# Last FFN: VectorE adds the right tap through PSUM, ScalarE rounds in two activations

## The chip, the core and the metric

The kernel runs on one NeuronCore of a Trainium2 chip. TensorE (PE in the profile) multiplies matrices and writes into PSUM, VectorE (DVE) and GpSimd (POOL) do elementwise work and reductions, ScalarE (ACT) evaluates activations, SyncE (SP) issues most of the DMAs. GpSimd cannot reach PSUM. Every engine runs its own instructions in order, and the engines hold each other back only by semaphores. The metric is the device time of one execution in microseconds, median of several runs.

## The reference, cut to what matters

The kernel computes one decoder layer on x of 4 x 1024 x 512 (4096 tokens): x = x + attention(norm(x)), x = x + cross block(norm(x), ctx), x = x + ffn(norm(x)). The change lies in the last of the three:

```python
def _L0_ffn_ref(x, w1, conv_w, conv_b, w2):      # w1 2048x512, w2 512x2048
    def act_quant(x):
        scale = 127.0 / jnp.clip(jnp.max(jnp.abs(x), axis=-1, keepdims=True), 1e-05)
        return jnp.clip(jnp.round(x * scale), -128, 127) / scale
    ...
    h = bit_linear(x, w1)                        # both operands quantised, then x @ w1.T
    h = depthwise_conv1d(h.transpose(0, 2, 1), conv_w, conv_b)   # 3 taps along the tokens
    h = h.transpose(0, 2, 1)
    h = jax.nn.silu(h)
    return bit_linear(h, w2)
```

Each token's scale needs the largest |h| over all 2048 hidden columns before h can be rounded and multiplied by w2.

## The kernel before, in words

The program is a chain of stages. The last, `quantised_ffn`, finds the rounded x, both rounded weights and their units ready in DRAM. It works on half a sequence at a time: 8 units of 512 tokens, each with 16 blocks of 128 hidden columns, so 128 blocks of 128 partitions (hidden columns) x 512 tokens. A block i passes these steps:

- PE `block_product` (L2411): four matmuls of 512 columns into `acc`, two PSUM banks in turn.
- DVE `dequantise` (L2534): `acc` times the tokens' units gives `y`, two buffers.
- ACT `set_edge` (L2488): one column of `y`; ACT `centre` (L2495): middle tap plus bias, into PSUM; ACT `right_tap` (L2499).
- DVE `add_left` (L2543): left tap plus `centre` gives `conv`; POOL `add_right` (L2375): plus `right_tap`.
- ACT `silu` (L2479): `conv` gives `h`, kept for two whole units.
- PE `turn` (L2420): four transposes of `h` into `turned`, one PSUM bank with no second buffer; DVE `find_max` (L2551): the largest of each token in the block.
- After a unit's 16 blocks DVE `scales` (six small instructions up to `diag`, L2557 to L2568), PE `spread_scale` (L2428) and an ACT copy (L2513) make `scale_row`.
- POOL `scale_block` (L2381): `h` times `scale_row`; DVE `round_block` (L2576): adds and takes away 1.5 x 2^23, written as bf16 into `hqT`; PE `w2_product` (L2438); DVE `finish` (L2584) once in four blocks.
- Every second unit PE has 128 one-column products for the next sequence's edges (L2402).

All engines are written by the same loop over slots s. In slot s each engine handles block s - lag of each of its steps, with the lags in a few constants, and the order inside a slot is the order of the calls. In slot s PE runs `block_product(s)`, a `w2_product`, and `turn(s - TURN_AT)`; DVE runs `find_max(s - MAX_AT)`, `dequantise(s)`, `add_left(s - 1)`, `round_block`. Buffers tie the blocks: `turn(i)` waits for `maxed` of block i - 1, since `turned` has one buffer:

```python
pe.wait_ge(silu_done, i + 1)
past(pe, maxed, i)
```

and `dequantise(i)` waits for `h_ready` of block i. PE reaches `block_product(s + 1)` only when it is through with `turn(s - TURN_AT)`.

Of the kernel before, what the change touches and what calls it, by code (L numbers as in the profile page):

```python
# [27 lines left out]
ALU = mybir.AluOpType  # L28
# [3 lines left out]
P = 128  # L32
# [2203 lines left out]
def quantised_ffn(nc, ident, w1T_parts, conv_w, conv_b, w2T_parts, w_mean, x2_rows, xq_parts, x_units, out_rows):  # L2236
# [9 lines left out]
    SILU_AT, TURN_AT, MAX_AT = 3, 4, 5  # L2246
    SPREAD_AT, SCALE_AT, ROUND_AT = HB + 5, HB + 6, HB + 7
# [3 lines left out]
    with ExitStack() as ctx:  # L2251
# [13 lines left out]
        right_tap = sb("right_tap", [P, 2, HALF])  # L2265
# [23 lines left out]
        centre_ready, right_ready = sem("centre_ready"), sem("right_ready")  # L2289
# [4 lines left out]
        h_scaled_ready, hq_ready = sem("h_scaled_ready"), sem("hq_ready")  # L2294
        out_ready, out_done = sem("out_ready"), sem("out_done")
# [26 lines left out]
        with nc.Block() as block:  # L2322
# [37 lines left out]
            def _(pool):  # L2360
# [3 lines left out]
                pool.memset(ones[:, :], 1.0).then_inc(const_step, 1)  # L2364
                for s in range(2):
                    pool.memset(y[:, 0, s, 0:1], 0.0).then_inc(const_step, 1)
                    pool.memset(y[:, 1, s, HALF + 1:], 0.0).then_inc(const_step, 1)
                pool.wait_ge(small_loaded, 32)
                pool.wait_ge(const_step, 5)
                pool.sem_inc(const_step, 1)  # L2370

                def add_right(i):
                    pool.wait_ge(right_ready, i + 1)
                    pool.wait_ge(left_added, i + 1)
                    pool.tensor_tensor(conv[:, i % CR], conv[:, i % CR], right_tap[:, i % 2], ALU.add).then_inc(right_added, 1)  # L2375

                def scale_block(i):
                    u, f = divmod(i, HB)
                    pool.wait_ge(scale_row_ready, u + 1)
                    past(pool, hq_ready, i - 1)  # L2380
                    pool.tensor_tensor(h_scaled[:, i % 2], h[:, u % 2, f], scale_row[:, u % 2], ALU.mult).then_inc(h_scaled_ready, 1)  # L2381

                for s in range(END):
# [3 lines left out]
                    i = block_at(s, 1)  # L2387
                    if i is not None:
                        add_right(i)

            @block.tensor
            def _(pe):
                pe.wait_ge(const_step, 6)
# [69 lines left out]
                for f in range(HB):  # L2463
                    pe.wait_ge(hq_ready, LAST * HB + f + 1)
# [6 lines left out]
            def _(act):  # L2471
                act.wait_ge(const_step, 6)
# [7 lines left out]

                def set_edge(i):
# [4 lines left out]
                    past(act, right_ready, i - 1)  # L2486
# [3 lines left out]
                def taps_of(i):  # L2490
# [3 lines left out]
                    past(act, left_added, i - 1)  # L2494
                    act.activation(centre[:, i % 2], y[:, s, i % 2, 1:HALF + 1], ACT.Identity, bias=conv_bias[:, f:f + 1],  # L2495
                                   scale=taps[:, f, 1:2]).then_inc(centre_ready, 1)
                    past(act, right_added, i - 1)
                    act.wait_ge(y_edged, i + 1)
                    act.activation(right_tap[:, i % 2], y[:, s, i % 2, 2:HALF + 2], ACT.Identity, scale=taps[:, f, 2:3])\  # L2499
                        .then_inc(right_ready, 1)  # L2500

                for s in range(END):
                    if s < SLOTS:
                        set_edge(s)
                        taps_of(s)
                    i = block_at(s, SILU_AT)
                    if i is not None:
                        silu(i)
# [160 lines left out]
```

## Time and profile before

| | before |
|---|---|
| median of 3 runs | 3545.81 us (3543.29 to 3549.79) |
| the profiled execution's own time | 3542.34 us |
| its span | 3540.7 us |
| mean granted TensorE clock | 0.962 |
| busy over the span: PE, DVE, ACT, POOL | 3167.0, 2344.0, 1767.6, 1171.8 us |
| last stage, first to last block's `y` | 3107.53 to 3477.52 us |

The span runs from the first to the last instruction; the own time of that execution is 1.64 us more. Busy shares over the whole span mix all stages; the change touches only the instructions after about 3090 us. In the rows below, a window's row has its start and end, its length, the busy time of PE, PEld (weight load), DVE, ACT and POOL with their counts, the granted clock of TensorE as a share of full speed (1.00 is 2.4 GHz, 0.50 is 1.2 GHz), the DMA share and GB/s. A group's row has line, engine, operation, output<-inputs, shapes and count, then busy us and mean ns of one, then idle us before it and who ended it. A timeline's row has start, duration, engine, line, operation, output<-inputs, and in brackets the idle time before it with its releaser.

### The profile page before, as it was taken

What the parts mean: (1) busy time and instruction counts of PE and PEld (TensorE: products, weight loads), DVE (VectorE), ACT (ScalarE), POOL (GpSimd) and SP (SyncE); (2) the same over time, 40 slices, a digit from 0 to 9 for tenths busy, and PEclk for the clock granted to TensorE, in tenths of its full rate; (3) what the DMA queues carried; (4) which work ended last, traced back from release to release, by engine and by line L of the source; (5) the groups of instructions that cost most, each with busy time, mean ns of one, the idle gap of its engine ahead of it and who ended that gap; (6) DMA issues with size and microseconds to landing.
All of it is one profiled execution on the core that took longest, in us unless ns stands there. A gap on an engine that the chain in (4) does not pass through costs nothing. (4 is left out here: it accounts for less than half of the span.)

```text
span 3540.7 us, 57138 instructions
## 1 busy us (share of the span) xinstructions
PE 3167.0 (89%) x19234; PEld 2282.3 (64%) x19234; DVE 2344.0 (66%) x4197; ACT 1767.6 (50%) x3130; POOL 1171.8 (33%) x901
## 2 busy tenths in 40 slices
PE   6998999999999999789996998599999999368886
PEld 5776666666666666567775777487877788334443
DVE  5562788888888888644553888634445444379996
ACT  3331888888888888522323222132222222076662
POOL 2343311312231132144442455300111111058886
PEclk9999999999999999999998999799999999689999
DMA  6775311321222122355645443321111110201112
GB/s 216 239 243 169 85 60 56 92 62 56 73 79 61 56 85 68 122 181 188 228 171 184 129 131 118 108 84 42 42 42 43 42 42 29 82 22 55 60 42 72
DMA packets 239351, 350.53 MB, mean 99 GB/s; under 512 B 31792, under 2 KB 129104, under 8 KB 239184
## 3 DMA queue, kind: packets, MB, share of 16 engines
q1 hardware_dynamic: 208256, 290.41, 25.5%
q0 software_dynamic: 8912, 32.82, 2.8%
q10 hardware_dynamic: 22016, 25.17, 2.0%
q8 instruction: 93, 1.52, 0.2%
q14 instruction: 74, 0.61, 0.1%
HBM read 210.68 MB, written 137.64 MB: 98 GB/s over the span
## 5 line engine op out<-in xcount | busy, mean ns | idle before, releaser
L887 DVE CUSTOM_DVE_ANT_0 attend_scores<-attend_scores,attend_bias_table 128x1024 f32<-128x1024 f32 x512 | 630.5, 1232 | 164.8 <-PE attend_scores L741 161.5
L814 ACT ACTIVATE attend_probs<-attend_scores,attend_neg_max 128x1024 f32<-128x1024 f32 x512 | 571.7, 1117 | 141.0 <-DVE attend_neg_max L887 131.3
L753 PE MATMUL attend_turned<-ident,attend_probs 128*128 128x128 f32 x4096 | 557.3, 275 | 12.6 <-DVE attend_probsT L895 12.5
L753 PEld LDWEIGHTS attend_turned<-ident,attend_probs 128*128 128x128 f32 x4096 | 472.9, 141 | 121.4 <-DVE attend_probsT L895 30.2
L741 PE MATMUL attend_scores<-attend_k_stack,attend_q_stack 96*128 96x512 f32 x1024 | 373.4, 446 | 18.1 <-DMA attend_q_stack<-qk_parts 15.0
L822 ACT COPY attend_probsT<-attend_turned 128x512 f32<-128x512 f32 x640 | 359.5, 583 | 24.7 <-PE attend_turned L753 23.1
L2217 DVE TENSOR_TENSOR cross_ffn_h_lo<-cross_ffn_hidden,cross_ffn_h_hi 128x512 fp32r<-128x512 f32 x128 | 95.8, 753 | 363.7 <-ACT cross_ffn_h_hi L2114 363.1
L703 POOL TENSOR_TENSOR attend_out_parts<-attend_out_full,attend_out_parts 128x256 fp32r<-128x256 f32 x64 | 46.6, 727 | 847.3 <-ACT attend_out_parts L829 847.3
L768 PE MATMUL attend_out_acc<-attend_probsT,attend_v_in 128*32 128x256 f32 x4096 | 312.9, 389 | 0.7 <-DVE attend_out_full L905 0.7
L741 PEld LDWEIGHTS attend_scores<-attend_k_stack,attend_q_stack 96*128 96x128 f32 x1024 | 154.1, 190 | 175.2 <-issue 154.8
L895 DVE COPY attend_probsT<-attend_turned 128x512 f32<-128x512 f32 x384 | 263.5, 686 | 1.3 <-PE attend_turned L753 1.3
L2111 ACT ACTIVATE cross_ffn_hidden<-cross_ffn_h_acc,cross_ffn_b_cols 128x512 f32<-128x512 f32 x128 | 88.2, 689 | 266.3 <-PE cross_ffn_h_acc L2028 250.1
L697 POOL TENSOR_TENSOR attend_bias_table<-attend_neg_distance,attend_slope_now 128x1920 f32<-128x1920 f32 x64 | 214.8, 3388 | 1.4
L2026 PE MATMUL cross_ffn_h_acc<-cross_ffn_aT_hi,cross_ffn_w_hi 128*128 128x512 f32 x512 | 203.6, 398 | 5.6 <-issue 5.6
L2375 POOL TENSOR_TENSOR quantised_ffn_conv<-quantised_ffn_conv,quantised_ffn_right_tap 128x512 f32<-128x512 f32 x128 | 178.4, 1394 | 88.8 <-DVE quantised_ffn_conv L2543 88.8
L2039 PE MATMUL cross_ffn_out_acc<-cross_ffn_w_hi,cross_ffn_h_hi 128*128 128x512 f32 x512 | 206.3, 403 | 1.1 <-DVE cross_ffn_h_lo L2217 0.6
L2027 PE MATMUL cross_ffn_h_acc<-cross_ffn_aT_hi,cross_ffn_w_lo 128*128 128x512 f32 x512 | 202.9, 396 | 0.0
L2114 ACT CAST cross_ffn_h_hi<-cross_ffn_hidden 128x512 fp32r<-128x512 f32 x128 | 79.5, 621 | 247.1 <-PE cross_ffn_out_acc L2041 246.1
L2028 PE MATMUL cross_ffn_h_acc<-cross_ffn_aT_lo,cross_ffn_w_hi 128*128 128x512 f32 x512 | 202.5, 396 | 0.0
L2040 PE MATMUL cross_ffn_out_acc<-cross_ffn_w_lo,cross_ffn_h_hi 128*128 128x512 f32 x512 | 202.3, 395 | 0.0
L2041 PE MATMUL cross_ffn_out_acc<-cross_ffn_w_hi,cross_ffn_h_lo 128*128 128x512 f32 x512 | 202.3, 395 | 0.0
L2381 POOL TENSOR_TENSOR quantised_ffn_h_scaled<-quantised_ffn_h,quantised_ffn_scale_row 128x512 f32<-128x512 f32 x128 | 164.2, 1285 | 12.3 <-ACT quantised_ffn_scale_row L2513 7.6
(294 smaller groups left out, 6644.5 us busy)
## 6 DMA issues: line engine op xcount, KB each, us to landing
qk_parts<-qkv_qk_out SPq DMA_DIRECT2D x64, 512.0 KB, 3.2
attend_k_stack<-qk_parts SPq DMA_DIRECT2D x192, 128.0 KB, 2.5
attend_q_stack<-qk_parts SPq DMA_DIRECT2D x192, 128.0 KB, 2.7
qkv_wq_raw<-L_ffn_w POOLq DMA_DIRECT2D x16, 1024.0 KB, 7.6
o_parts<-attend_out_parts ACTq DMA_DIRECT2D x64, 256.0 KB, 2.5
carried_o_in<-o_parts SPq DMA_DIRECT2D x32, 512.0 KB, 6.5
qkv_x_in<-x SPq DMA_DIRECT2D x8, 1024.0 KB, 5.7
v_rows<-qkv_v_out SPq DMA_DIRECT2D x32, 256.0 KB, 3.4
```

Source lines behind the costliest of these rows:

```text
L697: pool.tensor_tensor(bias_table[:, h], neg_distance[:, :], slope_now[:, h:h + 1].to_broadcast([P, SPAN]), ALU.mult).then_inc(table_ready, 1)
L741: last = pe.matmul(scores[:, i % 2, k * HALF:(k + 1) * HALF], q_stack[:, h, queries], k_stack[:, h, k * HALF:(k + 1) * HALF], start=True, ...
L753: last = pe.transpose(turned[:, x, c], probs[:, i % 2, k * P:(k + 1) * P], ident[:, :])
L768: last = pe.matmul(out_acc[rows, 0:QG], v_in[:, c, rows], probsT[:, (qg - 1) % 2, c, h], start=(c == 0), stop=(c == TB - 1))
L814: act.activation(probs[:, i % 2], scores[:, i % 2], ACT.Exp, bias=neg_max[:, i % 4:i % 4 + 1], scale=-1.0, accum_out=den[:, qg % 2, j, h:h ...
L822: act.copy(probsT[:, qg % 2, x * HB:(x + 1) * HB, h, j * P:(j + 1) * P], turned[:, x]).then_inc(copied[x], 1)
L887: dve.tensor_tensor_reduce(scores[:, i % 2], scores[:, i % 2], bias_table[:, h, at:at + T], -1.0, BIG, ALU.add, ALU.min, neg_max[:, i % 4: ...
L895: dve.tensor_copy(probsT[:, qg % 2, HB:TB, h, j * P:(j + 1) * P], turned[:, 1]).then_inc(copied[1], 1)
L2026: pe.matmul(out, w1_hi[:, c, cols], aT_hi[:, c], start=c == 0, stop=False)
L2027: pe.matmul(out, w1_lo[:, c, cols], aT_hi[:, c], start=False, stop=False)
L2028: last = pe.matmul(out, w1_hi[:, c, cols], aT_lo[:, c], start=False, stop=c == KB - 1)
L2039: pe.matmul(out_acc[:, t], hi, w2_hi[:, j], start=j == 0, stop=False)
```

## The change

The right tap moves from ACT and POOL to DVE: `add_left` now writes its sum back into `centre` in PSUM, and a new DVE `add_right` adds the right tap to it and writes `conv`. POOL keeps only `scale_block`. The rounding moves from DVE to ACT for the first seven units: one Identity activation with a bias column of +1.5 x 2^23 written in place into `h_scaled` (`round_up`), and one with the negative bias into `hqT` (`round_down`), with `silu` between the two. The last unit's 16 blocks are still rounded by DVE (`round_last`). All lags from `silu` on are one slot smaller, and on DVE `find_max` moves from the head of the slot to the place between `add_left` and `add_right`.

```diff
-    SILU_AT, TURN_AT, MAX_AT = 3, 4, 5
-    SPREAD_AT, SCALE_AT, ROUND_AT = HB + 5, HB + 6, HB + 7
+    SILU_AT, TURN_AT, MAX_AT = 2, 3, 4
+    SPREAD_AT, SCALE_AT, ROUND_AT = HB + 4, HB + 5, HB + 6
...
-                def add_right(i):
-                    pool.wait_ge(right_ready, i + 1)
-                    pool.wait_ge(left_added, i + 1)
-                    pool.tensor_tensor(conv[:, i % CR], conv[:, i % CR], right_tap[:, i % 2], ALU.add).then_inc(right_added, 1)
...
+                def round_up(i):
+                    act.wait_ge(h_scaled_ready, i + 1)
+                    act.activation(h_scaled[:, i % 2], h_scaled[:, i % 2], ACT.Identity, bias=round_up_col[:, :]).then_inc(h_raised, 1)
+
+                def round_down(i):
+                    u, f = divmod(i, HB)
+                    act.wait_ge(h_raised, i + 1)
+                    if f == 0:
+                        past(act, out_ready, (u - 1) * HT)
+                    act.activation(hqT[:, u % 2, f], h_scaled[:, i % 2], ACT.Identity, bias=round_down_col[:, :]).then_inc(hq_ready, 1)
...
-                    past(act, right_added, i - 1)
-                    act.wait_ge(y_edged, i + 1)
-                    act.activation(right_tap[:, i % 2], y[:, s, i % 2, 2:HALF + 2], ACT.Identity, scale=taps[:, f, 2:3])\
-                        .then_inc(right_ready, 1)
...
+                    dve.scalar_tensor_tensor(out=centre[:, i % 2], in0=y[:, u % 2, i % 2, 0:HALF], scalar=taps[:, f, 0:1], in1=centre[:, i % 2],
+                                             op0=ALU.mult, op1=ALU.add).then_inc(left_added, 1)
+
+                def add_right(i):
+                    u, f = divmod(i, HB)
+                    dve.wait_ge(left_added, i + 1)
                     past(dve, silu_done, i - CR + 1)
-                    dve.scalar_tensor_tensor(out=conv[:, i % CR], in0=y[:, u % 2, i % 2, 0:HALF], scalar=taps[:, f, 0:1], in1=centre[:, i % 2],
-                                             op0=ALU.mult, op1=ALU.add).then_inc(left_added, 1)
+                    dve.scalar_tensor_tensor(out=conv[:, i % CR], in0=y[:, u % 2, i % 2, 2:HALF + 2], scalar=taps[:, f, 2:3], in1=centre[:, i % 2],
+                                             op0=ALU.mult, op1=ALU.add).then_inc(right_added, 1)
...
                 for s in range(END):
-                    i = block_at(s, MAX_AT)
-                    if i is not None:
-                        find_max(i)
                     if s < SLOTS:
                         dequantise(s)
                     i = block_at(s, 1)
                     if i is not None:
                         add_left(i)
+                    i = block_at(s, MAX_AT)
+                    if i is not None:
+                        find_max(i)
+                    i = block_at(s, 1)
+                    if i is not None:
+                        add_right(i)
                     i = block_at(s, ROUND_AT)
-                    if i is not None:
-                        round_block(i)
+                    if i is not None and i >= LAST * HB:
+                        round_last(i - LAST * HB)
```

On DVE, at the start of the stage's loop, the order before around the first two `find_max` (`block_max`) is this; the rows ahead of it hold the first four blocks' `y` and three `conv`:

```order
L2534 TENSOR_TENSOR quantised_ffn_y<-quantised_ffn_acc,quantised_ffn_unit_row 128x512
L2543 SCALAR_TENSOR_TENSOR quantised_ffn_conv<-quantised_ffn_y,quantised_ffn_taps,quantised_ffn_centre 128x512
L2551 TENSOR_REDUCE quantised_ffn_block_max<-quantised_ffn_turned 128x4
L2534 TENSOR_TENSOR quantised_ffn_y<-quantised_ffn_acc,quantised_ffn_unit_row 128x512
L2543 SCALAR_TENSOR_TENSOR quantised_ffn_conv<-quantised_ffn_y,quantised_ffn_taps,quantised_ffn_centre 128x512
L2551 TENSOR_REDUCE quantised_ffn_block_max<-quantised_ffn_turned 128x4
```

The same place after the change, with the line numbers of the changed kernel:

```order
L2544 TENSOR_TENSOR quantised_ffn_y<-quantised_ffn_acc,quantised_ffn_unit_row 128x512
L2552 SCALAR_TENSOR_TENSOR quantised_ffn_centre<-quantised_ffn_y,quantised_ffn_taps,quantised_ffn_centre 128x512
L2567 TENSOR_REDUCE quantised_ffn_block_max<-quantised_ffn_turned 128x4
L2559 SCALAR_TENSOR_TENSOR quantised_ffn_conv<-quantised_ffn_y,quantised_ffn_taps,quantised_ffn_centre 128x512
L2544 TENSOR_TENSOR quantised_ffn_y<-quantised_ffn_acc,quantised_ffn_unit_row 128x512
L2552 SCALAR_TENSOR_TENSOR quantised_ffn_centre<-quantised_ffn_y,quantised_ffn_taps,quantised_ffn_centre 128x512
L2567 TENSOR_REDUCE quantised_ffn_block_max<-quantised_ffn_turned 128x4
```

Both start with the fifth block's `y`, block 4. Before, the first max (block 0) stood at the head of slot 5, ahead of block 5's `y`. Now it stands in slot 4, behind `y` of block 4 and the left tap of block 3, and ahead of `add_right`.

On PE, the start of the loop before; x20 are the products of five blocks (slots 0 to 4), and the transposes of `turn` follow:

```order
L2411 MATMUL quantised_ffn_acc<-quantised_ffn_xqT,quantised_ffn_w1T 128x512 x20
L2420 MATMUL quantised_ffn_turned<-ident,quantised_ffn_h 128x128 x4
L2411 MATMUL quantised_ffn_acc<-quantised_ffn_xqT,quantised_ffn_w1T 128x512 x4
L2420 MATMUL quantised_ffn_turned<-ident,quantised_ffn_h 128x128 x4
L2411 MATMUL quantised_ffn_acc<-quantised_ffn_xqT,quantised_ffn_w1T 128x512 x4
```

And after the change:

```order
L2409 MATMUL quantised_ffn_acc<-quantised_ffn_xqT,quantised_ffn_w1T 128x512 x16
L2418 MATMUL quantised_ffn_turned<-ident,quantised_ffn_h 128x128 x4
L2409 MATMUL quantised_ffn_acc<-quantised_ffn_xqT,quantised_ffn_w1T 128x512 x4
L2418 MATMUL quantised_ffn_turned<-ident,quantised_ffn_h 128x128 x4
L2409 MATMUL quantised_ffn_acc<-quantised_ffn_xqT,quantised_ffn_w1T 128x512 x4
```

One block's product fewer stands ahead of the first `turn`: the product of block 4 now comes behind the transposes of block 0, and so on to the end, one `turn` between any two products.

## Rows read from the trace of the kernel before

**Rows 1.** Window from the first block's `y` to the last block's, last stage.

```profile
3107.53:3477.52 369.99, 295.27 (x1761) 151.68 (x1760) 341.33 (x548) 259.63 (x512) 302.24 (x231) 0.95 0.13 42
```

**Rows 2.** Groups of instructions between 3270 and 3298 us, about ten slots.

```profile
L2375 POOL TENSOR_TENSOR quantised_ffn_conv<-quantised_ffn_conv,quantised_ffn_right_tap 128x512 f32<-128x512 f32 x10 | 14.2, 1417 | 1.2 <-DVE quantised_ffn_conv L2543 1.2
L2381 POOL TENSOR_TENSOR quantised_ffn_h_scaled<-quantised_ffn_h,quantised_ffn_scale_row 128x512 f32<-128x512 f32 x11 | 14.1, 1286 | 0.0
...
L2495 ACT ACTIVATE quantised_ffn_centre<-quantised_ffn_y,quantised_ffn_conv_bias,quantised_ffn_taps 128x512 f32<-128x512 f32 x11 | 8.6, 782 | 7.4 <-DVE quantised_ffn_y L2534 7.4
L2543 DVE SCALAR_TENSOR_TENSOR quantised_ffn_conv<-quantised_ffn_y,quantised_ffn_taps,quantised_ffn_centre 128x512 f32<-128x512 f32 x11 | 8.1, 732 | 0.0
L2551 DVE TENSOR_REDUCE quantised_ffn_block_max<-quantised_ffn_turned 128x4 f32<-128x512 f32 x11 | 7.5, 679 | 0.0
L2576 DVE TENSOR_SCALAR quantised_ffn_hqT<-quantised_ffn_h_scaled 128x512 bf16<-128x512 f32 x10 | 7.5, 747 | 0.0
L2534 DVE TENSOR_TENSOR quantised_ffn_y<-quantised_ffn_acc,quantised_ffn_unit_row 128x512 f32<-128x512 f32 x11 | 7.5, 678 | 0.1
L2499 ACT ACTIVATE quantised_ffn_right_tap<-quantised_ffn_y,quantised_ffn_taps 128x512 f32<-128x512 f32 x10 | 7.1, 706 | 0.0
...
L2479 ACT ACTIVATE quantised_ffn_h<-quantised_ffn_conv 128x512 f32<-128x512 f32 x10 | 6.1, 613 | 0.0
```

**Rows 3.** Groups, 3030 to 3541 us: the same rounding in the stage before.

```profile
L2206 DVE TENSOR_SCALAR cross_ffn_xq<-cross_ffn_xn 128x512 bf16<-128x512 f32 x4 | 1.7, 428 | 0.1
```

**Rows 4.** Timeline of the first slots, where the granted clock is low from 3116 us.

```profile
3107.53 0.69 DVE L2534 TENSOR_TENSOR quantised_ffn_y<-quantised_ffn_acc,quantised_ffn_unit_row 128x512 f32<-128x512 f32 x1 [9.51 <-PE quantised_ffn_acc L2411]
...
3118.78 1.06 PE L2420 MATMUL quantised_ffn_turned<-ident,quantised_ffn_h 128*128 128x128 f32 x4
3119.22 0.69 DVE L2534 TENSOR_TENSOR quantised_ffn_y<-quantised_ffn_acc,quantised_ffn_unit_row 128x512 f32<-128x512 f32 x1 [1.21 <-PE quantised_ffn_acc L2411]
3119.63 1.91 PE L2411 MATMUL quantised_ffn_acc<-quantised_ffn_xqT,quantised_ffn_w1T 128*128 128x512 bf16 x4
3119.82 0.74 DVE L2543 SCALAR_TENSOR_TENSOR quantised_ffn_conv<-quantised_ffn_y,quantised_ffn_taps,quantised_ffn_centre 128x512 f32<-128x512 f32 x1
...
3120.48 0.69 DVE L2551 TENSOR_REDUCE quantised_ffn_block_max<-quantised_ffn_turned 128x4 f32<-128x512 f32 x1
...
3121.78 0.69 DVE L2534 TENSOR_TENSOR quantised_ffn_y<-quantised_ffn_acc,quantised_ffn_unit_row 128x512 f32<-128x512 f32 x1 [0.61 <-PE quantised_ffn_acc L2411]
```

**Rows 5.** Timeline of two places at the full granted clock.

```profile
3125.00 1.03 PE L2411 MATMUL quantised_ffn_acc<-quantised_ffn_xqT,quantised_ffn_w1T 128*128 128x512 bf16 x4
...
3126.26 0.69 DVE L2534 TENSOR_TENSOR quantised_ffn_y<-quantised_ffn_acc,quantised_ffn_unit_row 128x512 f32<-128x512 f32 x1 [0.37 <-PE quantised_ffn_acc L2411]
...
3277.18 0.68 DVE L2551 TENSOR_REDUCE quantised_ffn_block_max<-quantised_ffn_turned 128x4 f32<-128x512 f32 x1
...
3278.01 0.63 PE L2420 MATMUL quantised_ffn_turned<-ident,quantised_ffn_h 128*128 128x128 f32 x4 [0.32 <-DVE quantised_ffn_block_max L2551]
...
3278.48 1.03 PE L2411 MATMUL quantised_ffn_acc<-quantised_ffn_xqT,quantised_ffn_w1T 128*128 128x512 bf16 x4
```

**Rows 6.** Windows with their granted clock: in the second stage, then in unit 0.

```profile
355.00:363.00 8.00, 3.73 (x10) 2.56 (x11) 2.76 (x5) 2.39 (x4) 8.00 (x4) 0.50 1.05 246
3122.00:3138.00 16.00, 10.62 (x57) 5.44 (x57) 14.44 (x23) 13.92 (x29) 8.89 (x7) 1.00 0.00 0
```

**Rows 7.** Groups, 3030 to 3541 us: PE's edge products and spreads of the last stage.

```profile
L2402 PE MATMUL quantised_ffn_spread<-quantised_ffn_xqT,quantised_ffn_w1T 128*128 128x1 bf16 x512 | 13.7, 164 | 26.1 <-DMA quantised_ffn_w1T<-w1T_parts 26.1
...
L2428 PE MATMUL quantised_ffn_spread<-quantised_ffn_diag,quantised_ffn_ones 128*128 128x512 f32 x16 | 12.0, 846 | 3.0 <-DVE quantised_ffn_diag L2568 3.0
```

**Rows 8.** Timeline: first of the `scales` instructions, the max behind the last.

```profile
3298.84 0.20 DVE L2557 TENSOR_REDUCE quantised_ffn_h_max<-quantised_ffn_block_max 128x4 f32<-128x64 f32 x1
...
3302.14 0.69 DVE L2551 TENSOR_REDUCE quantised_ffn_block_max<-quantised_ffn_turned 128x4 f32<-128x512 f32 x1
```

**Rows 9.** Timeline: first two scalings of the last unit on POOL.

```profile
3494.36 2.49 POOL L2381 TENSOR_TENSOR quantised_ffn_h_scaled<-quantised_ffn_h,quantised_ffn_scale_row 128x512 f32<-128x512 f32 x2 [3.17 <-ACT quantised_ffn_scale_row L2513]
```

More of the change, by code:

```diff
@@ L2264, in quantised_ffn @@
         conv = sb("conv", [P, CR, HALF])
-        right_tap = sb("right_tap", [P, 2, HALF])
+        round_up_col = sb("round_up_col", [P, 1])
+        round_down_col = sb("round_down_col", [P, 1])
         block_max = sb("block_max", [P, HT, HB])
@@ L2364, in _ @@
                 pool.memset(ones[:, :], 1.0).then_inc(const_step, 1)
+                pool.memset(round_up_col[:, :], ROUND).then_inc(const_step, 1)
+                pool.memset(round_down_col[:, :], -ROUND).then_inc(const_step, 1)
                 for s in range(2):
@@ L2379, in scale_block @@
                     pool.wait_ge(scale_row_ready, u + 1)
-                    past(pool, hq_ready, i - 1)
+                    if u == LAST and f >= 2:
+                        pool.wait_ge(last_hq_ready, f - 1)
+                    else:
+                        past(pool, hq_ready, i - 1)
                     pool.tensor_tensor(h_scaled[:, i % 2], h[:, u % 2, f], scale_row[:, u % 2], ALU.mult).then_inc(h_scaled_ready, 1)
@@ L2463, in _ @@
                 for f in range(HB):
-                    pe.wait_ge(hq_ready, LAST * HB + f + 1)
+                    pe.wait_ge(last_hq_ready, f + 1)
                     for t in range(HT):
@@ L2471, in _ @@
             def _(act):
-                act.wait_ge(const_step, 6)
+                act.wait_ge(const_step, 8)
                 def silu(i):
@@ L2505, in _ @@
                         taps_of(s)
+                    r = block_at(s, ROUND_AT)
+                    if r is not None and r < LAST * HB:
+                        round_up(r)
                     i = block_at(s, SILU_AT)
@@ L2508, in _ @@
                         silu(i)
+                    if r is not None and r < LAST * HB:
+                        round_down(r)
                     u = half_at(s, SPREAD_AT)
@@ L2529, in dequantise @@
                     past(dve, centre_ready, i - 1)
-                    past(dve, right_ready, i - 1)
+                    past(dve, right_added, i - 1)
                     past(dve, left_added, i - 1)
@@ L2569, in scales, with round_last @@
                                       h_scale[:, :].unsqueeze(2).to_broadcast([P, HT, P]), ALU.mult).then_inc(diag_ready, 1)
-                def round_block(i):
-                    u, f = divmod(i, HB)
+                def round_last(f):
+                    i = LAST * HB + f
                     dve.wait_ge(h_scaled_ready, i + 1)
                     if f == 0:
-                        past(dve, out_ready, (u - 1) * HT)
-                    dve.tensor_scalar(hqT[:, u % 2, f], h_scaled[:, i % 2], ROUND, -ROUND, ALU.add, ALU.add).then_inc(hq_ready, 1)
+                        past(dve, out_ready, (LAST - 1) * HT)
+                    dve.tensor_scalar(hqT[:, LAST % 2, f], h_scaled[:, i % 2], ROUND, -ROUND, ALU.add, ALU.add).then_inc(last_hq_ready, 1)
                 def finish(j):
```

16 lines of the change are left out of this document (7 added, 9 removed).

## Prediction

> **What bounds the kernel now.** I read the windows first: the change touches only the last stage, and its 128 slots, from the first block's `y` to the last block's, take 370.0 us, 2.9 us a slot [rows 1]. No DMA matters there (0.13 busy). Then the groups of a steady piece, to see which engine fills a slot. POOL does: one `conv` of 1417 ns and one `h_scaled` of 1286 ns are 2.70 us, with 1.2 us of idle time in about 28 [rows 2]. DVE has 0.73 + 0.68 + 0.75 + 0.68 = 2.84 us of busy time a slot, but neighbouring instructions overlap by about 0.07 us, so it is as full as POOL. The two also hold each other up: the rounding to bf16 takes 747 ns beside POOL's work, and 428 ns in the same shape and types where POOL has nothing to do [rows 3]. ACT has 0.78 + 0.71 + 0.61 us and waits for `y` 7.4 us of the 28 [rows 2]. So before the change, sums of work set the pace, and PE's and the buffers' chains of waits lie just under it.
>
> The Trainium skill (SBUF, State Buffer, on the shared port pair) says that a VectorE operation in a two-port mode and a GpSimd operation exclude each other for a whole instruction. The trace agrees (747 against 428 ns), and by this rule alone the change would pay, since it takes this kind of instruction off DVE and halves POOL's work. That result is the first rival below.
>
> **What the change does to the sums.** Off POOL: 1.42 us a slot. Off ACT: `right_tap`, 0.71. Off DVE: the rounding, 0.75. On DVE: a second tap, priced as the first, 0.73 (its source in PSUM is the same kind; the first tap's *output* now goes to PSUM, which no DVE row shows; between nothing and the 0.08 us by which `centre`, which writes PSUM, exceeds `right_tap`; I take nothing). On ACT: two activations, each like `right_tap` at 0.71 or like `silu` at 0.61. So a slot costs DVE about 2.6 to 2.7 us, ACT 0.17 + 0.78 + 0.71 + 0.61 + 0.71 less overlaps, some 2.6, POOL 1.29. Sums alone would say "about as before".
>
> **What it does to the chains.** The question is what a slot must wait for in turn. Before, `find_max` was DVE's first instruction of a slot. After it PE could turn, then multiply block s+1, and the result was wanted only by the second DVE instruction of the next slot; one trip around that chain covered two slots. Now DVE runs, in slot s, `y(s)`, left tap of s-1, max of s-4, right tap. PE's `turn(s-3)` waits for the max of block s-4 (one buffer in `turned`), `block_product(s+1)` stands behind this turn, and `y(s+1)` waits for the product. The max of the next slot stands behind `y(s+1)`. So the chain product, `y`, left tap, max, turn, product closes within one slot, and every slot costs its whole length. `acc` has two buffers, but PE's order doesn't let it use the second.
>
> Each link has a row. At the full clock: product start to `y` start where `y` waits for it, 3125.00 to 3126.26, 1.26 us [rows 5]; `y` to left tap 0.60 and left tap to max 0.66 (3119.22, 3119.82, 3120.48) [rows 4]; max start to the turn that waits for it 0.83 (3277.18 to 3278.01); turn to product 0.47 (3278.01 to 3278.48) [rows 5]. Together 3.82 us a slot. At the low clock two links grow: product to `y` 2.15 (3119.63 to 3121.78), turn to product 0.85 (3118.78 to 3119.63) [rows 4]: 5.09 us. The right tap and, once in four slots, `finish` lie behind the max and are hidden: the next `y` comes 0.83 + 0.47 + 1.26 = 2.56 us after the max started, and max, right tap and `finish` together need some 0.6 + 0.65 + 0.74 = 2.0. The `w2_product` lies between a product and the turn, where PE waits anyway. ACT's 2.6 and POOL's 1.3 us fit in the slot.
>
> **Which clock.** The turn of block 0 waits for the first `silu`, and there the clock had fallen before: a product took 1.91 us [rows 4] where it takes 1.03 at the full clock [rows 5]. In units 0 and 1 up to slot 35 there is no `w2_product` yet, so PE has about 2.8 us of work in 5.09 and then waits. The nearest rows: a stretch of 8 us with PE busy 3.73 us stayed at 0.50, and one of 16 us with PE busy 10.62 us stayed at 1.00 [rows 6]. I take the low clock for slots 4 to 36, and the full one from there: with the `w2_product` PE is busy at the low clock nearly all the time, which brings it up, and then about 2.4 us in 3.82, the share of the second row. The Trainium skill (TensorE: Matmul & The Clock Gate, on what is happening) says the same in general: half rate is the default, and activity releases it. It can't say which side this slot falls on; by the row of 0.50 the first two units cost 5.09 a slot, by the other 3.82.
>
> **The sum**, from the first `y` to the last:
> - Start to `y(4)`: the first `y` behind a turn came at 3119.22, 11.7 us after the first; it now comes one slot earlier. I take 10.0 us (between 7 and 11.7).
> - 33 slots at 5.09: 168.0. 90 slots at 3.82: 343.8.
> - Spreads and edge products stand in PE's queue between a turn and the next product, so they are on the chain in full: 16 records of 846 ns are 1.7 us for each of 8 spreads; six at the full clock, one at the low one at double: 13.6. Edge products: 13.7 us for four times, 3.4 each; three times: 10.2 [rows 7].
> - `scales` follow the right tap: 3.3 us with POOL in their way [rows 8], I take 2.0 with POOL idle two thirds of the time. 0.6 + 0.65 + 2.0 against the 2.56 that the slot waits anyway: 0.7, six times, 4.2.
> - The clock falls once after each of the two later edge products: 2 x 1.27 = 2.5.
>
> 552.3 us against 370.0: +182.3. Behind the last `y`: before, POOL's first scaling of the last unit started 16.8 us after it (3494.36 less 3477.52) [rows 9, 1]. Now four maxes at some 1.7, the scales, the spread and the copy make 11.5, ACT's rounding of the six blocks left about 12; I take 12.4, 4.4 us saved. What follows (16 scalings and roundings by POOL and DVE, the last products) is unchanged. In sum +177.9 us on the profiled execution's 3542.3: 3720. That execution was 3.5 below the median of the runs, so I say **3724**, 5.0% slower.
>
> **The rivals.**
> - The full clock holds in all slots (0.14): 9.5 + 123 x 3.82 + 7 x 1.7 + 10.2 + 7 x 0.7 = 506.4, +136.4 - 4.4 = +132: 3678. For it: the clock was full at the start of the loop. Against it: PE would then have 1.5 us of work in 3.8. A mixture of both lies between.
> - The low clock holds to the end of the loop (0.04): 90 x 1.27 = 114 more: 3838. Against it: rows 6, second row.
> - Only the sums of work count, by the port rule (0.05): if PE's product of block s+1 did not have to wait for the max of its own slot, DVE would set the pace: 0.60 + 0.66 + 0.60 + 0.78 (the next `y` waits for the right tap's end) = 2.64 a slot, 127 x 2.64 + 22 x 0.66 for `finish` + 7 x 2.0 for `scales` = 364, -6; with the end -10.4: 3535, faster. It decides from the point at which max and turn are early enough for the product, 1.2 us a slot. Against it: the order of PE's rows, in which a turn stands between any two products, and the wait of the turn for the max before it.
> - The chain closes in part only, because one wait is met earlier than I think, or the new PSUM output and ACT's two roundings add a little (0.06): from no change to +90, 3540 to 3640.
>
> **How the numbers follow.** My case has 0.71, with 3700 to 3745: its ends are 0.08 us a slot for PSUM output (+10), the start (3), the scales (6) and some slots of the first units at the full clock (to -25). The range for 8 in 10 takes in the full clock: 3670 to 3748. Slower by over 0.2% (7 us, about what a measurement of this kernel can tell from no change): 0.71 + 0.14 + 0.04 + 0.05 of the last rival, 0.94. Faster: 0.04 of the third rival. Within 0.2%: what is left of these two, 0.02.
>
> **What the changed profile would show.** Between 3250 and 3450 us slots of 3.8 us, every `y` waiting for PE's product, every turn for `block_max`, POOL idle two thirds of the time, DVE's busy share down from 0.92 to about 0.75; in unit 0 slots of 5.1 us at clock 0.50; no DVE rounding longer than 0.45 us ahead of the last unit, and the last `y` near 3660 us. The forecast is wrong if `y` waits for the right tap or ACT instead, if slots are under 3 us, or if the clock in unit 0 is 1.00.

## The result and the profile after

The changed kernel takes 3722.76 us (median of 4 runs, 3719.88 to 3727.76) against 3544.94 us before (4 runs): ratio 1.0505, 95% interval 1.0491 to 1.052. The forecast was 3724, range 3670 to 3748. The profiled execution took 3727.76 us, with a span of 3725.8.

Three windows of the kernel after: from the first block's `y` to the last block's (the counterpart of [rows 1]), a piece of unit 0, and a later piece with `w2_product` in it.

```profile
3115.19:3665.52 550.33, 335.61 (x1746) 164.61 (x1767) 357.85 (x569) 314.49 (x597) 134.57 (x107) 0.83 0.09 28
3140.00:3180.00 40.00, 22.34 (x64) 10.42 (x64) 19.84 (x32) 11.91 (x24) 0.00 (x0) 0.50 0.00 0
3380.00:3420.00 40.00, 26.13 (x120) 12.40 (x120) 27.94 (x45) 26.88 (x51) 12.68 (x10) 0.93 0.20 66
```

The loop grew by 180.3 us, from 370.0 to 550.3. DVE, the fullest engine before, has 357.85 us of work in it, which is 0.65 of the stretch. No engine is full any more. In the third window the granted clock is 0.93 because its first slot, up to 3384.19 us, still ran at the low clock; from 3390 us on it is 1.00. What fills the slots is waiting. These are rows of the list of who waited for whom in the kernel after, 3110 to 3660 us (total us, times, longest):

```profile
POOL quantised_ffn_h_scaled L2383 <- ACT quantised_ffn_hqT L2488: 282.9, 97, 7.1
ACT quantised_ffn_centre L2504 <- DVE quantised_ffn_y L2544: 223.1, 125, 9.7
...
DVE quantised_ffn_y L2544 <- PE quantised_ffn_acc L2409: 198.0, 118, 9.2
PE quantised_ffn_turned L2418 <- DVE quantised_ffn_block_max L2567: 165.4, 104, 2.8
```

The last two close a ring: `y` waits for the product, the turn for the max, and the product stands behind the turn, the max behind `y`. One trip around it in the timeline of the kernel after, steady part:

```profile
3403.30 0.69 DVE L2544 TENSOR_TENSOR quantised_ffn_y<-quantised_ffn_acc,quantised_ffn_unit_row 128x512 f32<-128x512 f32 x1 [1.22 <-PE quantised_ffn_acc L2409]
3403.91 0.75 DVE L2552 SCALAR_TENSOR_TENSOR quantised_ffn_centre<-quantised_ffn_y,quantised_ffn_taps,quantised_ffn_centre 128x512 f32<-128x512 f32 x1
...
3404.56 0.69 DVE L2567 TENSOR_REDUCE quantised_ffn_block_max<-quantised_ffn_turned 128x4 f32<-128x512 f32 x1
...
3405.39 0.63 PE L2418 MATMUL quantised_ffn_turned<-ident,quantised_ffn_h 128*128 128x128 f32 x4 [1.47 <-DVE quantised_ffn_block_max L2567]
3405.86 1.03 PE L2409 MATMUL quantised_ffn_acc<-quantised_ffn_xqT,quantised_ffn_w1T 128*128 128x512 bf16 x4
...
3407.12 0.69 DVE L2544 TENSOR_TENSOR quantised_ffn_y<-quantised_ffn_acc,quantised_ffn_unit_row 128x512 f32<-128x512 f32 x1 [1.22 <-PE quantised_ffn_acc L2409]
```

0.61 + 0.65 + 0.83 + 0.47 + 1.26 = 3.82 us from `y` to `y`. The same ring in unit 0, where the granted clock is 0.50:

```profile
3124.83 0.69 DVE L2544 TENSOR_TENSOR quantised_ffn_y<-quantised_ffn_acc,quantised_ffn_unit_row 128x512 f32<-128x512 f32 x1 [1.57 <-PE quantised_ffn_acc L2409]
...
3126.09 0.69 DVE L2567 TENSOR_REDUCE quantised_ffn_block_max<-quantised_ffn_turned 128x4 f32<-128x512 f32 x1
3126.28 0.61 ACT L2477 ACTIVATE quantised_ffn_h<-quantised_ffn_conv 128x512 f32<-128x512 f32 x1
...
3126.93 1.09 PE L2418 MATMUL quantised_ffn_turned<-ident,quantised_ffn_h 128*128 128x128 f32 x4 [2.33 <-ACT quantised_ffn_h L2477]
...
3127.81 1.91 PE L2409 MATMUL quantised_ffn_acc<-quantised_ffn_xqT,quantised_ffn_w1T 128*128 128x512 bf16 x4
3129.95 0.69 DVE L2544 TENSOR_TENSOR quantised_ffn_y<-quantised_ffn_acc,quantised_ffn_unit_row 128x512 f32<-128x512 f32 x1 [2.52 <-PE quantised_ffn_acc L2409]
```

5.12 us: `y` to max 1.26, max to turn 0.84, turn to product 0.88, product to `y` 2.14. A trap in reading stands in the turn's row. The releaser named is the `silu` that ended at 3126.89, but this is the second turn, that of block 1, and that `silu` is the third, block 2's. What the turn wanted of ACT was ready earlier; it started 0.84 us after the max, where the turns labelled with the max start after 0.83. 19 turns in the first units carry the label of ACT. Only the first of them, block 0's at 3122.40 us, really waited for its `silu`, which ended at 3122.34; the other 18 have the same 2.33 us of idle time as this one.

The operations themselves cost what was assumed. Groups of the kernel after, 3110 to 3660 us:

```profile
L2383 POOL TENSOR_TENSOR quantised_ffn_h_scaled<-quantised_ffn_h,quantised_ffn_scale_row 128x512 f32<-128x512 f32 x105 | 132.9, 1266 | 436.0 <-ACT quantised_ffn_hqT L2488 282.9 <-ACT quantised_ffn_scale_row L2523 153.1
...
L2552 DVE SCALAR_TENSOR_TENSOR quantised_ffn_centre<-quantised_ffn_y,quantised_ffn_taps,quantised_ffn_centre 128x512 f32<-128x512 f32 x125 | 93.4, 747 | 0.0
L2559 DVE SCALAR_TENSOR_TENSOR quantised_ffn_conv<-quantised_ffn_y,quantised_ffn_taps,quantised_ffn_centre 128x512 f32<-128x512 f32 x125 | 92.4, 739 | 0.1
...
L2481 ACT ACTIVATE quantised_ffn_h_scaled<-quantised_ffn_h_scaled,antised_ffn_round_up_col 128x512 f32<-128x512 f32 x104 | 73.4, 706 | 0.0
L2488 ACT ACTIVATE quantised_ffn_hqT<-quantised_ffn_h_scaled,tised_ffn_round_down_col 128x512 bf16<-128x512 f32 x103 | 72.5, 704 | 0.0
```

The tap that writes PSUM takes 747 ns and the one that writes SBUF 739; the roundings on ACT take 706 and 704 as `right_tap` did.

### The profile page after: what moved, and what is told of

It is laid out like the page before. It is cut to its first block and busy times, and to the rows that moved or that the text cites. A ratio compares the mean times of both kernels' runs of the same rounds, so it can differ in the third digit from the quotient of the medians.

```text
span 3725.8 us, 56845 instructions
## 1 busy us (share of the span) xinstructions
PE 3217.5 (86%) x19209; PEld 2303.4 (62%) x19234; DVE 2354.6 (63%) x4213; ACT 1828.7 (49%) x3226; POOL 998.1 (27%) x775
## 5 line engine op out<-in xcount | busy, mean ns | idle before, releaser
L2418 PE MATMUL quantised_ffn_turned<-ident,quantised_ffn_h 128*128 128x128 f32 x512 | 94.0, 314 | 215.1 <-DVE quantised_ffn_block_max L2567 169.2
L2418 PEld LDWEIGHTS quantised_ffn_turned<-ident,quantised_ffn_h 128*128 128x128 f32 x512 | 62.4, 158 | 288.5 <-issue 226.8
L2544 DVE TENSOR_TENSOR quantised_ffn_y<-quantised_ffn_acc,quantised_ffn_unit_row 128x512 f32<-128x512 f32 x128 | 88.6, 692 | 200.7 <-PE quantised_ffn_acc L2409 200.5
L2504 ACT ACTIVATE quantised_ffn_centre<-quantised_ffn_y,quantised_ffn_conv_bias,quantised_ffn_taps 128x512 f32<-128x512 f32 x128 | 100.0, 781 | 225.5 <-DVE quantised_ffn_y L2544 225.5
```

The lines of the kernel that those rows point to most:

```text
L2418: last = pe.transpose(turned[:, t], h[:, u % 2, f, t * P:(t + 1) * P], ident[:, :])
```

## Experiments

The theory: the ring of product, `y`, left tap, max, turn sets each slot, and where the ring is open the sums of work return. Rivals: the moved work itself costs the time; only the low clock of the first units does. e3 to e7 are two executions each, the others five to twelve; every ratio is to executions of the kernel before taken beside them, whose medians were 3545.34 us for e1 to e4, 3543.37 for e5 to e8 and 3542.69 for e9 and e10.

**e1, PE's product one slot ahead.** The changed kernel with one edit:

```diff
+                block_product(0)
                 for s in range(END):
-                    if s < SLOTS:
-                        block_product(s)
+                    if s + 1 < SLOTS:
+                        block_product(s + 1)
```

> The changed kernel, with one thing moved: TensorE runs the product of block s+1 in slot s, ahead of the transposes, instead of at the head of slot s+1. The instructions and their number stay. Theory (the chain product, y, left tap, max, turn, product closes in one slot): with the product ahead of the turn one trip of that chain covers two slots, 1.91 us each, so VectorE's work sets the pace, 2.64 us a slot; no slot of 5.1 us is left in the first two units; the stage's 127 slots take 360 to 370 us instead of 550 and the time is 3530 to 3545. Rival (the second tap on VectorE, its output in PSUM or the two activations are what costs): the same work, so the slots stay near 3.8 us and the time stays within 20 of 3723.

Measured: 3545.52 us, ratio to before 1.0001 (0.9993 to 1.001). DVE's timeline of this kernel:

```profile
3224.25 0.69 DVE L2545 TENSOR_TENSOR quantised_ffn_y<-quantised_ffn_acc,quantised_ffn_unit_row 128x512 f32<-128x512 f32 x1
3224.86 0.75 DVE L2553 SCALAR_TENSOR_TENSOR quantised_ffn_centre<-quantised_ffn_y,quantised_ffn_taps,quantised_ffn_centre 128x512 f32<-128x512 f32 x1
3225.51 0.69 DVE L2568 TENSOR_REDUCE quantised_ffn_block_max<-quantised_ffn_turned 128x4 f32<-128x512 f32 x1
3226.11 0.74 DVE L2560 SCALAR_TENSOR_TENSOR quantised_ffn_conv<-quantised_ffn_y,quantised_ffn_taps,quantised_ffn_centre 128x512 f32<-128x512 f32 x1
3226.95 0.69 DVE L2545 TENSOR_TENSOR quantised_ffn_y<-quantised_ffn_acc,quantised_ffn_unit_row 128x512 f32<-128x512 f32 x1
```

DVE is back to back at 2.70 us a slot, and nothing is left of the 178 us. All the moved work is still in this kernel. The rest of the distance to 2.64 is the last gap, 0.84 us where 0.78 was taken: the next `y` waits for the end of the right tap just before it. The loop takes 373.3 us, 3 more than the expectation's upper end, and the time is 0.5 above its range. Both misses are small beside the rival's 3723.

**e2, the old lags and the max at the head of the slot again**, with all the moved work:

```diff
-    SILU_AT, TURN_AT, MAX_AT = 2, 3, 4
-    SPREAD_AT, SCALE_AT, ROUND_AT = HB + 4, HB + 5, HB + 6
+    SILU_AT, TURN_AT, MAX_AT = 3, 4, 5
+    SPREAD_AT, SCALE_AT, ROUND_AT = HB + 5, HB + 6, HB + 7
...
                 for s in range(END):
+                    i = block_at(s, MAX_AT)
+                    if i is not None:
+                        find_max(i)
                     if s < SLOTS:
                         dequantise(s)
...
                         add_left(i)
-                    i = block_at(s, MAX_AT)
-                    if i is not None:
-                        find_max(i)
-                    i = block_at(s, 1)
                     if i is not None:
                         add_right(i)
```

> The changed kernel with the lags and the place of find_max of the kernel before (lags 3, 4, 5, the max at the head of VectorE's slot); right tap and rounding stay on VectorE and ScalarE. Theory: the chain again covers two slots; VectorE pays one more dependence (the right tap follows the left tap at once), 0.60 + 0.61 + 0.78 + 0.78 = 2.77 us a slot, and the time is 3540 to 3560. Rival (the moved work costs, not the order): it stays within 20 of 3723.

Measured: 3544.91 us, ratio 0.9996 (0.9987 to 1.0005); `y` to `y` 370.3 us, 2.64 a slot. The expectation had 2.77, since it charged the max for a wait that only the right tap has. After one wait of ACT both DVE and ACT are back to back (the rows show `y` to `y` and `centre` to `centre`, 2.65 and 2.64 us):

```profile
3223.68 0.68 DVE L2544 TENSOR_TENSOR quantised_ffn_y<-quantised_ffn_acc,quantised_ffn_unit_row 128x512 f32<-128x512 f32 x1
...
3224.41 0.78 ACT L2504 ACTIVATE quantised_ffn_centre<-quantised_ffn_y,quantised_ffn_conv_bias,quantised_ffn_taps 128x512 f32<-128x512 f32 x1 [0.66 <-DVE quantised_ffn_y L2544]
...
3226.33 0.68 DVE L2544 TENSOR_TENSOR quantised_ffn_y<-quantised_ffn_acc,quantised_ffn_unit_row 128x512 f32<-128x512 f32 x1
...
3227.05 0.78 ACT L2504 ACTIVATE quantised_ffn_centre<-quantised_ffn_y,quantised_ffn_conv_bias,quantised_ffn_taps 128x512 f32<-128x512 f32 x1
```

So the work moved by the change is worth nothing either way as long as the ring is open.

**e3, the order alone.** The kernel before, its work where it was, with only the six lags from `silu` on one smaller and `find_max` behind `add_left`.

> The kernel before with nothing but the lags 2, 3, 4 and find_max behind the left tap; the right tap stays on ScalarE and GpSimd and the rounding on VectorE. Theory: this alone closes the chain, slots of 3.82 us (5.1 at the low clock in the first units), time 3705 to 3730. Rival (the moved work costs): within 15 of 3545.

Measured: 3728.9 us, ratio 1.0515 (1.0495 to 1.0535), `y` to `y` 562.4 us, slots of 5.12 up to slot 35 and of 3.82 after. The order alone gives the whole loss. The lags and the place of the max were only ever changed together (e2, e3), so what either is worth by itself is not shown. Rows of this kernel show that DVE's rounding, at 1.19 us longer than the mean in [rows 2], is hidden in the ring; the next `y` still comes 2.56 us after the max, as after the change:

```profile
3402.35 0.69 DVE L2551 TENSOR_REDUCE quantised_ffn_block_max<-quantised_ffn_turned 128x4 f32<-128x512 f32 x1
3402.58 1.27 POOL L2375 TENSOR_TENSOR quantised_ffn_conv<-quantised_ffn_conv,quantised_ffn_right_tap 128x512 f32<-128x512 f32 x1 [0.84 <-DVE quantised_ffn_conv L2543]
3402.95 1.19 DVE L2576 TENSOR_SCALAR quantised_ffn_hqT<-quantised_ffn_h_scaled 128x512 bf16<-128x512 f32 x1
3404.91 0.69 DVE L2534 TENSOR_TENSOR quantised_ffn_y<-quantised_ffn_acc,quantised_ffn_unit_row 128x512 f32<-128x512 f32 x1 [0.77 <-PE quantised_ffn_acc L2411]
```

**e4, PE filled in the first slots.** The changed kernel with four more matmuls a slot up to slot 35, whose results nothing reads:

```diff
+                    elif s < PRODUCT_AT:
+                        for f in range(4):
+                            pe.matmul(out_acc[:, s % 2], w1T[:, 0, f * P:(f + 1) * P], w2T[:, f], start=f == 0, stop=f == 3)
```

> The changed kernel with four more 512-column matmuls a slot on TensorE in slots 0 to 35, where there is no w2 product; their result is not read. The chain stays closed. Theory: they lie where TensorE waits, keep its granted clock at 1.00 there, and the slots of 5.1 us become 3.82; 127 slots take 505 to 515 us instead of 550, time 3680 to 3690. Rival (the first units are slow for another reason than the clock): no change from 3723, or slower by the added matmuls.

Measured: 3687.19 us (3683.51 to 3690.87), ratio 1.0397 (1.0377 to 1.0418). The same window of the kernel after and then of this one:

```profile
3120.00:3240.00 120.00, 64.86 (x314) 31.53 (x314) 63.16 (x103) 42.72 (x83) 7.55 (x6) 0.57 0.00 1
```

```profile
3120.00:3240.00 120.00, 75.85 (x483) 38.98 (x490) 79.73 (x129) 60.88 (x118) 18.97 (x15) 0.99 0.05 18
```

More work on PE made the kernel 36 us faster: the granted clock stays up, slots are 3.82 us from slot 4 on, and `y` to `y` falls from 550.3 to 515.8 us. That is the price of the low clock in the first two units; the other 146 us of the loop's loss stand at the full clock.

**e5, the max directly behind `y`.** The changed kernel; the ring is one left tap (0.66) shorter:

```diff
                     if s < SLOTS:
                         dequantise(s)
-                    i = block_at(s, 1)
-                    if i is not None:
-                        add_left(i)
                     i = block_at(s, MAX_AT)
                     if i is not None:
                         find_max(i)
                     i = block_at(s, 1)
                     if i is not None:
+                        add_left(i)
                         add_right(i)
```

> The changed kernel with find_max straight behind y, ahead of the left tap; lags and everything else as in the change. The left tap drops out of the closed chain. Theory: a slot at the full clock is shorter by the left tap's share, 1.26 + 0.60 + 0.83 + 0.47 = 3.16 us instead of 3.82, at the low clock 4.43 instead of 5.1; time 3605 to 3650. Rival (a slot's length comes from VectorE's or ScalarE's work or from the PSUM output): the same work, so 3.82 us and 3723 stay.

Measured: 3616.53 us (3609.48 to 3623.57), ratio 1.0206 (1.0186 to 1.0225), `y` to `y` 440.7 us. DVE's timeline of this kernel:

```profile
3351.89 0.69 DVE L2544 TENSOR_TENSOR quantised_ffn_y<-quantised_ffn_acc,quantised_ffn_unit_row 128x512 f32<-128x512 f32 x1 [0.43 <-PE quantised_ffn_acc L2409]
3352.50 0.68 DVE L2567 TENSOR_REDUCE quantised_ffn_block_max<-quantised_ffn_turned 128x4 f32<-128x512 f32 x1
3353.10 0.75 DVE L2552 SCALAR_TENSOR_TENSOR quantised_ffn_centre<-quantised_ffn_y,quantised_ffn_taps,quantised_ffn_centre 128x512 f32<-128x512 f32 x1
3353.88 0.75 DVE L2559 SCALAR_TENSOR_TENSOR quantised_ffn_conv<-quantised_ffn_y,quantised_ffn_taps,quantised_ffn_centre 128x512 f32<-128x512 f32 x1
3355.05 0.69 DVE L2544 TENSOR_TENSOR quantised_ffn_y<-quantised_ffn_acc,quantised_ffn_unit_row 128x512 f32<-128x512 f32 x1 [0.42 <-PE quantised_ffn_acc L2409]
```

3.16 us a slot, which is 3.82 less 0.66. The first units have it too, where 4.43 was expected at the low clock (see the last section). A sum of work would not have moved, since the same instructions run in another order.

**e6 and e7, each half of the moved work alone**, on the kernel before with its lags and order. e6 moves only the right tap to DVE (`add_left` into `centre`, `add_right` on DVE) and keeps the rounding there.

> Only the first part of the change with the lags and the order of before: VectorE adds the right tap through PSUM, and still rounds every block (ScalarE doesn't). Theory: the chain stays open, VectorE sets the pace with five instructions, 2.65 us as in the run with the max at the head plus 0.4 us for the rounding and what it waits for GpSimd, 3.0 to 3.4 a slot; time 3580 to 3640. Rival (the second tap is free, since GpSimd's halved work frees VectorE): 3545.

Measured: 3589.08 us (3586.91 to 3591.24), ratio 1.0128 (1.011 to 1.0147). One slot on DVE in this kernel:

```profile
3302.71 0.68 DVE L2536 TENSOR_TENSOR quantised_ffn_y<-quantised_ffn_acc,quantised_ffn_unit_row 128x512 f32<-128x512 f32 x1
3303.31 0.74 DVE L2544 SCALAR_TENSOR_TENSOR quantised_ffn_centre<-quantised_ffn_y,quantised_ffn_taps,quantised_ffn_centre 128x512 f32<-128x512 f32 x1
3304.09 0.75 DVE L2551 SCALAR_TENSOR_TENSOR quantised_ffn_conv<-quantised_ffn_y,quantised_ffn_taps,quantised_ffn_centre 128x512 f32<-128x512 f32 x1
3304.76 0.42 DVE L2584 TENSOR_SCALAR quantised_ffn_hqT<-quantised_ffn_h_scaled 128x512 bf16<-128x512 f32 x1
3305.09 0.68 DVE L2559 TENSOR_REDUCE quantised_ffn_block_max<-quantised_ffn_turned 128x4 f32<-128x512 f32 x1
3305.69 0.68 DVE L2536 TENSOR_TENSOR quantised_ffn_y<-quantised_ffn_acc,quantised_ffn_unit_row 128x512 f32<-128x512 f32 x1
```

DVE has five instructions and 2.98 us a slot, 2.65 plus 0.33 for a rounding that now takes 0.42 us. e7 moves only the rounding to ACT and keeps `right_tap` on ACT and `add_right` on POOL.

> Only the second part with the lags and the order of before: ScalarE rounds seven units in two activations, the right tap stays on ScalarE and GpSimd. Theory: ScalarE sets the pace: 0.09 + 0.72 + 0.61 + 0.52 + 0.61 + 0.61 = 3.16 us a slot, with little added for scales and finish, which ScalarE doesn't do; 127 slots 405 to 420 us, time 3575 to 3600. Rival (ScalarE has the room, POOL and VectorE gain by not excluding each other): 3530 to 3545.

Measured: 3564.69 us (3563.13 to 3566.25), ratio 1.006 (1.0041 to 1.0078): a miss by 10 us on the low side. ACT is back to back at 3.16 us a slot, as expected, but only once rounding has begun; up to about slot 23 two slots take 4.5 us together, which the expectation had not counted. Either half alone costs (46 and 21 us), the two together nothing.

**e8, e9 and e10, towards a faster version.** e8 is e2 with PE's edge products spread over eight slots instead of standing as one block of 128:

```diff
-                    if s % (2 * HB) == HB + 8 and s // (2 * HB) + 1 < B:
-                        edge_products(s // (2 * HB) + 1)
+                    k = s % (2 * HB) - (HB + 6)
+                    if 0 <= k < 8 and s // (2 * HB) + 1 < B:
+                        edge_products(s // (2 * HB) + 1, range(2 * k, 2 * k + 2))
...
-                    if s % (2 * HB) == HB + 9 and s // (2 * HB) + 1 < B:
+                    if s % (2 * HB) == HB + 14 and s // (2 * HB) + 1 < B:
                         find_edges(s // (2 * HB) + 1)
```

The last lines move the DVE step that reads these products five slots later.

> The kernel of e2 (change with the lags and order of before), with the 128 one-column edge products of a sequence spread over eight slots, 16 in each, instead of all in one. In e2 these slots last 5.2 to 6.1 us instead of 2.65, three times, and the one behind 0.8 more. Theory: the 0.43 us that each of eight slots gets on TensorE hides, 8 to 11 us less than e2: 3533 to 3538, ratio to before 0.997. Rival (another queue is late in those slots): as e2, 3545.

Measured: 3532.14 us (6 runs), ratio 0.997 (0.9958 to 0.9983), about 13 us below e2 and 0.9 below the expected range. e9 is the same edit on the kernel before, nothing else.

> The kernel before with one edit: PE's 128 edge products of the next sequence are issued in eight slots, 16 in each, and the DVE step that reads them stands six slots later. In the slots of these products the kernel before needs about 2.8 us more, three times. Theory (the edge products stand as a block in PE's queue, and in the kernel before as in the one with the open chain they hold the next product back): 3545 less about 8, 3536 (3533 to 3540), as the same edit took 12 us off the version with the max at the head of the slot. Rival (the edit pays only where ACT and DVE are freed by the rest of the change): 3543 to 3546, no difference.

Measured: 3536.15 us (11 runs), ratio 0.9982 (0.9973 to 0.9991). The edit gives the kernel before 6.5 us; e8 is 11.2 us below it, and the intervals of the two meet. So more than half of e8's gain is that edit, not the change, and the rest is not clear of the noise. e10 is e8 with `finish` of the first seven units split into an ACT scaling of the PSUM bank and a POOL addition of x2, and the edge column's copy on POOL:

```diff
+                def scale_out(j):
+                    u, t = divmod(j, HT)
...
+                    act.activation(out[:, j % 2], out_acc[:, j % 2], ACT.Identity, scale=h_unit[:, u % 3, t:t + 1]).then_inc(out_scaled, 1)
...
+                    pool.tensor_tensor(out[:, j % 2], out[:, j % 2], x2_in[:, j % 4], ALU.add).then_inc(out_done, 1)
```

> The version with the max at the head of the slot and the edge products spread, and with two more edits: finish (28 of 32 times) goes from DVE to ACT (scaling of the PSUM bank by the tokens' units) and POOL (adding x2), and the copy of one edge column goes from ACT to POOL. Theory (DVE bounds a slot at 2.64 us, with 0.66 more in every slot with a finish): DVE keeps 2.64 in all slots, 28 x 0.66 = 18 us less; ACT has 2.47 a slot and 0.61 more in one of four, 2.62 on average: 3532 less 10 to 18, 3514 to 3522. Rival one (ACT takes over as the bound in these slots, since it is as full as DVE at 2.64): 3528 to 3533. Rival two (POOL's copy of the edge comes late behind a scaling of 1.3 us, and the left tap waits for it): above 3535.

Measured: 3519.34 us (5 runs, 3514.47 to 3519.9), ratio 0.9934 (0.992 to 0.9947), `y` to `y` 349.3 us. A slot with a `finish` is no longer longer than the others. Timeline of this kernel across one, with the addition on POOL:

```profile
3400.61 1.27 POOL L2398 TENSOR_TENSOR quantised_ffn_out<-quantised_ffn_out,quantised_ffn_x_in 128x512 f32<-128x512 f32 x1
...
3401.15 0.68 DVE L2567 TENSOR_TENSOR quantised_ffn_y<-quantised_ffn_acc,quantised_ffn_unit_row 128x512 f32<-128x512 f32 x1
...
3403.80 0.68 DVE L2567 TENSOR_TENSOR quantised_ffn_y<-quantised_ffn_acc,quantised_ffn_unit_row 128x512 f32<-128x512 f32 x1
...
3406.44 0.68 DVE L2567 TENSOR_TENSOR quantised_ffn_y<-quantised_ffn_acc,quantised_ffn_unit_row 128x512 f32<-128x512 f32 x1
```

This is 0.7% faster than the kernel before and 5.5% faster than the kernel after. It uses what the change freed, POOL's time, but in the old order. That the split needs the change is argued from POOL's full slots before ([rows 2]); the split on the kernel before was not run.

## Why the prediction was right

**The ring.** Right in every link: 3.82 us predicted and measured at the full clock, 5.09 predicted and 5.12 measured at the low one. Shown from both sides: e3 closes it without the moved work and loses all, e1 and e2 open it with the moved work and lose nothing, e5 takes one link out and gains that link.

**The sums.** DVE 2.6 to 2.7 us: 2.64 in e2, 2.70 in e1. ACT "some 2.6": 2.64 in e2, no slack. "About as before" was right, and so was to price the PSUM output at nothing (8 ns).

**The clock.** Slots 4 to 36 were taken at the low clock. 24 of these 33 took 5.12 us and four 3.8 to 3.9; the other five carry scales, spreads or edge products. The 33 slots took 169.4 us with all that stands in them, where the sum has 168.0 and 8.5 more for two spreads and the first edge products. e4 shows the whole term of the low clock: 34.5 us, for the 41.9 (33 x 1.27) in the sum. The Trainium skill (TensorE: Matmul & The Clock Gate, on what is happening) has activity release the full rate. e4 agrees: with more matmuls the granted clock of the window is 0.99 in place of 0.57.

**The small terms**, each off by a little and in different directions. Start to `y(4)`: 9.6 for 10.0. In the 90 later slots, 371.3 us measured, 27.5 are above 3.82 each. Spreads give 9.4 for 8.5 and the two edge products 8.7 for 6.8; the two clock dips give 2.6 for 2.5. `scales` give 1.34 a time for 0.7, the one term that was off by a factor of two. Its `diag` row in the kernel after, and the next `y`:

```profile
3285.79 1.73 DVE L2584 TENSOR_TENSOR quantised_ffn_diag<-ident,quantised_ffn_h_scale 128x512 f32<-128x512 f32 x1
...
3287.45 0.68 DVE L2544 TENSOR_TENSOR quantised_ffn_y<-quantised_ffn_acc,quantised_ffn_unit_row 128x512 f32<-128x512 f32 x1
```

`diag` took 1.73 us here, and 1.73 or 1.74 in six of the seven units of the loop. It took 0.69 in the first (3203.96), before POOL's first scaling, and in the tail (3676.69), where POOL stood idle. POOL is idle two thirds of the time, as assumed, but here its one scaling of the slot starts just before it (3285.72, 1.26 us): in a ring the phases are fixed, and a share of idle time says nothing about which instruction meets which. In sum the 33 slots are 7 us below, the 90 slots 5.5 us above and the start 0.4 below: 550.3 for 552.3.

**The end.** From the last `y` to POOL's first scaling of the last unit: 3665.52 to this row of the kernel after, 13.7 us for the 12.4 taken.

```profile
3679.26 1.27 POOL L2383 TENSOR_TENSOR quantised_ffn_h_scaled<-quantised_ffn_h,quantised_ffn_scale_row 128x512 f32<-128x512 f32 x1 [2.63 <-ACT quantised_ffn_scale_row L2523]
```

The loop began 7.7 us later in this profile than in that of before (3115.19 against 3107.53), in stages that the change doesn't touch. Without it the profiled execution would have come out near 3720, as its sum did. The other runs are up to 7.9 us below the profiled one and left no trace, so where they differ is not known. That the median came within 1.3 us of 3724 is in part luck: terms of 7 us and 5.5 us missed in opposite directions. What the runs confirm is the ring and its length.

Two of the listed signs came out off: DVE's busy share between 3250 and 3450 us was 0.66 for "about 0.75" (131.72 of 200 us), and the last `y` stood at 3665.52 us for "near 3660", for the late start.

**The rivals.** Full clock throughout (3678): e4 is that case, made by hand, at 3687. Low clock to the end: not seen, slots are 3.82 from slot 37. The chain closed in part only, 3540 to 3640: not seen either, every plain slot has the whole ring. The rule of the Trainium skill (SBUF, State Buffer, on the shared port pair) that a two-port VectorE operation and a GpSimd operation exclude each other bears on the sums. The runs agree: the rounding took 1.19 us in e3, where it starts inside a POOL addition and ends 0.29 us after it (rows above), and 0.42 in e6, where POOL was idle around it (from 3302.94 to 3305.32). By this rule alone the change would have paid, but the sums didn't set the pace. Even with the ring open they gave nothing, since ACT, now at 2.64 us, and DVE took POOL's place. The 364 us that this rival gave the open loop left out the edge products: e2 took 370.3, and e8, with them spread, 361.9.

## What to carry to other kernels

Before moving work between engines, write down for one slot which instruction waits for which, in the order of every queue, and see whether that ring closes within the slot: it costs its whole length, whatever the busy shares say. An operation that releases another engine belongs ahead of the one that waits for that engine's next result; here one slot of lag and one place in a queue, together, were worth 178 us, and the moved work nothing. When such a change loses, try its order and its work apart: two short runs (e2, e3) settled it.

## What was not expected of the hardware

**The same matmuls a slot can stand at either clock.** e5 has the same PE work in a slot as the kernel after, in 3.16 us where that would need 3.82 at the full clock. Its window of the first units, to be set beside those at e4:

```profile
3120.00:3240.00 120.00, 63.53 (x419) 33.66 (x419) 95.17 (x149) 71.75 (x138) 24.03 (x19) 0.93 0.05 18
```

The granted clock was 0.93 with PE busy 63.53 of 120 us; the kernel after had 0.57 with 64.86. The busy times are nearly the same, but e5 got through 419 instructions in its time and the kernel after through 314, since each lasts longer at the low clock. What decides between the two levels is not shown by these runs, beyond that shorter slots (e5) and more matmuls in a slot (e4, 0.99) both stood at the high one for all or most of the window. The prediction took the low clock for all of these slots and met it here; for e5 the same reading missed.

**A DVE instruction that needs the result of the one just before it starts later.** Behind a left tap the max, which doesn't need it, starts after 0.65 us (e1, 3224.86 to 3225.51), and the right tap, which does, after 0.78 (e5, 3353.10 to 3353.88; e6, 3303.31 to 3304.09). In e1 `y`, whose buffer the right tap ahead of it releases, starts 0.84 us behind that tap's start. An independent instruction between would be worth 0.13 to 0.18 us a slot on a full engine. This is an estimate from these gaps: every order that kept DVE full has one such gap, and 2.64 (e2) against 2.70 us (e1) only shows which gap is the shorter.
